# First phase of a binarised-convolution block: centring in pairs with rings of four, reordered first operations, batch statistics aggregated in two parts

## The reference, cut to what matters

```python
x = x + conv_block(_ln_c(x))          # _ln_c: subtract the mean over channels, divide by the deviation
# conv_block:
xa = sign(x)                          # only the sign of the centred x matters
wc = clip(w - mean(w, over input channels), -1, 1)
alpha = mean(abs(wc), per output channel)
y = conv3x3(xa, sign(wc) * alpha, padding 1) + b
mean, var = y.mean((0, 2, 3)), y.var((0, 2, 3))     # over all 32 images
y = relu((y - mean) * rsqrt(var + 1e-5) * gamma + beta)
# then, per image: tokens t (3136 x 128)
t = t + ffn(layernorm(t))             # a router picks the best half of the tokens, a two-layer MLP runs, gated
```

## Time and profile before

| what | value |
|---|---|
| median of 3 runs | 2134.3 us (2131.57 to 2134.45) |
| the profiled execution's own time | 2142.42 us |
| its span | 2140.6 us |
| PE busy | 1998.0 us, 93% of the span |
| DVE busy | 1671.8 us, 78% |
| ACT busy | 1211.8 us, 57% |
| POOL busy | 934.4 us, 44% |
| mean rate of the DMA | 125 GB/s |

### The profile page before, as it was taken

The page is one execution under the profiler, slowest core; times in us unless marked ns, Lnnn a source line. Parts: engine busy times, 40 slices in busy tenths (PEclk is TensorE's granted clock), DMA queues, the critical chain, the costliest instruction groups (busy, mean ns, idle before and its releaser), DMA issues.

```text
span 2140.6 us, 35882 instructions
## 1 busy us (share of the span) xinstructions
PE 1998.0 (93%) x9515; PEld 1015.2 (47%) x9515; DVE 1671.8 (78%) x4759; ACT 1211.8 (57%) x2030; POOL 934.4 (44%) x714
## 2 busy tenths in 40 slices
PE   6999999996799999999999999999999999999995
PEld 3555555553344444544444444444444444444442
DVE  6777777775688888888888888888887888888875
ACT  3444444443466565666665666666666656666652
POOL 1000000002456555666565565556655656555543
PEclk9999999998899999999999999999999999999998
DMA  4343444443123333333333333332333333333213
GB/s 162 136 180 140 175 153 162 164 151 135 51 87 122 115 120 130 117 112 139 111 120 125 110 127 123 118 128 110 119 132 111 119 125 128 110 123 119 103 69 123
DMA packets 68726, 267.91 MB, mean 125 GB/s; under 512 B 22352, under 2 KB 27184, under 8 KB 64688
## 3 DMA queue, kind: packets, MB, share of 16 engines
q1 hardware_dynamic: 55264, 214.90, 27.5%
q10 hardware_dynamic: 13392, 52.29, 6.6%
HBM read 188.08 MB, written 77.87 MB: 124 GB/s over the span
## 4 chain that ended last, share of the span: by engine, by line
PE 47%; DMA 10%; SPq 6%; DVE 5%; issue 4%; POOL 1%; ACT 1%; ACTq 0%; POOLq 0%; DVEq 0%
PE ps L955 23%; PE ps L944 6%; DMA y<-y_int 5%; PE ps L946 5%; PE ps L945 5%; PE ps L900 5%; SPq L371 4%; DMA w_row<-wrow 3%; DMA wse<-w_row 3%; PE ps L933 2%; SPq L377 1%; DVE base L720 1%; ACT hs L500 1%; DVE rms L697 1%; DVE rms L694 1%
## 5 line engine op out<-in xcount | busy, mean ns | idle before, releaser
L955 PE MATMUL ps<-hs,w_c 128*128 128x448 f32 x1792 | 765.7, 554 | 0.6 <-ACT yo L510 0.6
L500 ACT ACTIVATE hs<-ps,b1c,undo 128x448 f32<-128x448 f32 x896 | 609.8, 719 | 127.4 <-PE ps L946 120.5
L871 PE MATMUL ps<-yo,cwT 128*128 128x448 bf16 x2016 | 425.3, 356 | 0.0
L955 PEld LDWEIGHTS ps<-hs,w_c 128*128 128x128 f32 x1792 | 314.0, 191 | 209.5 <-issue 176.0
L412 POOL TENSOR_TENSOR xb<-xb,zr 128x448 f32<-128x448 f32 x224 | 261.3, 1168 | 271.8 <-ACT zr L528 270.4
L417 POOL TENSOR_TENSOR tl<-tr,th 128x448 f16<-128x448 f32 x224 | 243.5, 1088 | 308.6 <-PE ps L946 192.7
L944 PE MATMUL ps<-th,w_h 128*128 128x448 f16 x896 | 318.4, 355 | 19.5 <-ACT hs L500 19.5
L946 PE MATMUL ps<-th,w_l 128*128 128x448 f16 x896 | 316.3, 353 | 0.0
L945 PE MATMUL ps<-tl,w_h 128*128 128x448 f16 x896 | 316.3, 353 | 0.0
L424 POOL TENSOR_TENSOR yo<-yo,base 128x448 f32<-128x448 f32 x224 | 279.7, 1255 | 77.1 <-DVE yo L797 77.1
L510 ACT ACTIVATE yo<-ps,cols 128x448 f32<-128x448 f32 x224 | 141.8, 633 | 237.9 <-PE ps L955 237.5
(11 more groups left out here) (125 smaller groups left out, 2355.1 us busy)
## 6 DMA issues: line engine op xcount, KB each, us to landing
xb<-x SPq DMA_DIRECT2D x31, 1568.0 KB, 7.5
xb<-x SPq DMA_DIRECT2D x33, 896.0 KB, 4.7
gate_all<-gate_row ACTq DMA_DIRECT2D x32, 896.0 KB, 4.4
result<-yo SPq DMA_DIRECT2D x32, 896.0 KB, 3.5
y_int<-y SPq DMA_DIRECT2D x32, 784.0 KB, 3.7
xb<-x SPq DMA_DIRECT2D x33, 672.0 KB, 4.4
gate_all<-gate_row ACTq DMA_DIRECT2D x32, 672.0 KB, 5.6
result<-yo SPq DMA_DIRECT2D x32, 672.0 KB, 3.0
```

The lines of the kernel that those rows point to most:

```text
L500: nc.scalar.activation(hs[(b + slot) % 2][:, j, :], ps[:, H_BANK + j, 0:T], ACT.Gelu_apprx_tanh, bias=b1c[:, j:j + 1], scale=undo[:, 1:2]) ...
L871: last = M(bank, cwT[:, t, :], sg[b][:, c * ROWS + dy:c * ROWS + dy + ROWS, dx:dx + SIDE], start=t == 0, stop=t == TAPS - 1)
L955: last = M(bank, w2_c[:, j, :], hs[(b + c) % 2][:, j, :], start=first, stop=final)
```

## The change

Three things are done, all in phase one and behind it.

1. The rings of xh and xl and the centring banks get four places, addressed by the chunk alone (c % 4); the banks are 0, 1, 4 and 5. ring_free gives the count of centrings (or signs) after which a place is free. newly_due names the chunks that are centred, and signed, after convolution c: none after an even c, two after an odd one, one after c = 6. DVE's order of splits stays as it was.
2. The start: PE centres chunks 0 and 1 ahead of the weights' transposes (which now use the convolution's banks), chunks 2 and 3 behind them, chunks 4 and 5 after the first convolution and 6 after the second. ACT's Abs moves behind the first four signs.
3. The statistics of images 0 to 29 are aggregated ahead of the last image's share of DVE's phase; behind it only the last two images' 14 chunks are. Six small operations join the two parts into one mean and variance.

```diff
+RING = 4
+        bn_early, bn_late, bn_apart = sm[:, 10:12], sm[:, 12:14], sm[:, 14:15]
+        EARLY = n_img - 2
-        xh = [sb(f"xh{b}", [C, T], f32r) for b in range(2)]
-        xl = [sb(f"xl{b}", [C, T], f32r) for b in range(2)]
+        xh = [sb(f"xh{q}", [C, T], f32r) for q in range(RING)]
+        xl = [sb(f"xl{q}", [C, T], f32r) for q in range(RING)]
-        CEN_BANK, CONV_BANK = 0, 2
+        CEN_BANKS, CONV_BANK = (0, 1, 4, 5), 2
+        def newly_due(c):
+            return (c - 1, c) if c % 2 else (c,) if c == NCH - 1 else ()
+
+        def ring_free(n, c):
+            if c >= RING:
+                return n * NCH + c - RING + 1
+            return (n - 1) * NCH + (c + RING if c + RING < NCH else c) + 1
...
         (ACT)
-            nc.scalar.activation(cwa, cwc, ACT.Abs, accum_out=abs_sum).then_inc(abs_summed, 1)
...
-                nc.scalar.activation(cwT[:, t, :], ps[:, t % 2, 0:C // 2].bitcast(bf16),
+                nc.scalar.activation(cwT[:, t, :], ps[:, CONV_BANK + t % 2, 0:C // 2].bitcast(bf16),
...
-                bank = CEN_BANK + (b + c) % 2
+                bank = CEN_BANKS[c % RING]
...
-            for c in range(NCH):
+            for c in range(RING):
                 sign(0, 0, c)
+            nc.scalar.activation(cwa, cwc, ACT.Abs, accum_out=abs_sum).then_inc(abs_summed, 1)
...
+                    if is_int(n) and n == 0 and c < 2:
+                        for k in (range(RING, NCH - 1), range(NCH - 1, NCH))[c]:
+                            sign(0, 0, k)
                     if has(n + 1):
-                        sign(n + 1, 1 - b, c)
+                        for k in newly_due(c):
+                            sign(n + 1, 1 - b, k)
...
         (DVE)
-                wait_count(dve, centred, g - 1)
-                V.tensor_copy(xh[(b + c) % 2][:, :], cut(xb[b], c)).then_inc(xh_ready, 1)
+                wait_count(dve, centred, ring_free(n, c))
+                V.tensor_copy(xh[c % RING][:, :], cut(xb[b], c)).then_inc(xh_ready, 1)
...
-            pairs(dve, phase1, 3, n_img - 1, 3, n_img)
-
+            pairs(dve, phase1, 3, n_img - 1, 3, n_img - 1)
+
+            dve.wait_ge(bn_taken, EARLY * NCH)
+            V.bn_aggr(bn_early, bnst[:, 0:EARLY * NCH, :])
+            phase1(n_img - 1, (n_img - 1) % 2)
             batch_stats(n_img - 1, (n_img - 1) % 2, NCH - 1)
 
             dve.wait_ge(bn_taken, n_img * NCH)
-            link(V.bn_aggr(bn_mv, bnst[:, :, :]))
+            link(V.bn_aggr(bn_late, bnst[:, EARLY * NCH:n_img * NCH, :]))
+            share = EARLY / n_img
+            link(V.tensor_tensor(bn_apart, bn_early[:, 0:1], bn_late[:, 0:1], ALU.subtract))
+            V.scalar_tensor_tensor(bn_mv[:, 0:1], bn_apart, share, bn_late[:, 0:1], ALU.mult, ALU.add)
+            link(V.scalar_tensor_tensor(bn_apart, bn_apart, share, bn_apart, ALU.mult, ALU.mult))
+            V.tensor_scalar(bn_early[:, 1:2], bn_early[:, 1:2], share, None, ALU.mult)
+            link(V.tensor_tensor(bn_late[:, 1:2], bn_late[:, 1:2], bn_apart, ALU.add))
+            link(V.scalar_tensor_tensor(bn_mv[:, 1:2], bn_late[:, 1:2], 1.0 - share, bn_early[:, 1:2], ALU.mult, ALU.add))
...
         (PE)
-                wait_count(pe, signed, g - 1)
-                bank = ps[:, CEN_BANK + (b + c) % 2, 0:T]
+                wait_count(pe, signed, ring_free(n, c))
+                bank = ps[:, CEN_BANKS[c % RING], 0:T]
...
-            for c in range(NCH):
+            pe.wait_ge(tables_ready, 2)
+            for c in range(2):
+                centre(0, 0, c)
+            pe.wait_ge(cw_signed, 1)
+            for t in range(TAPS):
+                wait_count(pe, cw_ready, t - 1)
+                nc.tensor.transpose(ps[:, CONV_BANK + t % 2, 0:C // 2].bitcast(bf16), cws[:, t, :],
+                                    ident_b[:, :]).then_inc(cw_transposed, 1)
+            pe.wait_ge(cw_ready, TAPS)
+            for c in range(2, RING):
                 centre(0, 0, c)
 
             def phase1(n, b):
                 for c in range(NCH):
                     conv(n, b, c)
+                    if is_int(n) and n == 0 and c < 2:
+                        for k in (range(RING, NCH - 1), range(NCH - 1, NCH))[c]:
+                            centre(0, 0, k)
                     if has(n + 1):
-                        centre(n + 1, 1 - b, c)
+                        for k in newly_due(c):
+                            centre(n + 1, 1 - b, k)
```

More of the change, by code:

```diff
@@ L556, in split @@
             def split(n, b, c):
-                g = n * NCH + c
                 if is_int(n) and n == 0:
@@ L563, in split @@
                     dve.wait_ge(x_in_s[b], (n - b) * 8 + 16)
-                wait_count(dve, centred, g - 1)
-                V.tensor_copy(xh[(b + c) % 2][:, :], cut(xb[b], c)).then_inc(xh_ready, 1)
+                wait_count(dve, centred, ring_free(n, c))
+                V.tensor_copy(xh[c % RING][:, :], cut(xb[b], c)).then_inc(xh_ready, 1)
             def split_low(n, b, c):
                 dve.wait_ge(xh_ready, n * NCH + c + 1)
-                V.tensor_tensor(xl[(b + c) % 2][:, :], cut(xb[b], c), xh[(b + c) % 2][:, :].bitcast(f32),
+                V.tensor_tensor(xl[c % RING][:, :], cut(xb[b], c), xh[c % RING][:, :].bitcast(f32),
                                 ALU.subtract).then_inc(split_ready, 1)
@@ L846, in _ @@
             M = nc.tensor.matmul
[L847 to L853, removed]
             def centre(n, b, c):
@@ L858, in centre @@
                 pe.wait_ge(split_ready, g + 1)
-                wait_count(pe, signed, g - 1)
-                bank = ps[:, CEN_BANK + (b + c) % 2, 0:T]
-                M(bank, centre_r[:, :], xh[(b + c) % 2][:, :], start=True, stop=False)
-                M(bank, centre_r[:, :], xl[(b + c) % 2][:, :], start=False, stop=True).then_inc(centred, 1)
+                wait_count(pe, signed, ring_free(n, c))
+                bank = ps[:, CEN_BANKS[c % RING], 0:T]
+                M(bank, centre_r[:, :], xh[c % RING][:, :], start=True, stop=False)
+                M(bank, centre_r[:, :], xl[c % RING][:, :], start=False, stop=True).then_inc(centred, 1)
             def conv(n, b, c):
```

## The result

The changed kernel takes 2124.1 us (median of 8 runs, 2118.7 to 2127.3) against 2134.4 for the kernel before (8 runs beside them, 2129.7 to 2140.3): the medians lie 10.3 us apart. The ratio of the two is given as 0.9943 with a 95% interval of 0.9928 to 0.9958; by it the kernel is 12.2 us faster (9.0 to 15.4), so the size of the gain is known to some 3 us only. Its profiled execution took 2127.27 us for a span of 2125.5, 15.1 less than the one of before.

A forecast was written before the change was run, and what follows sets the result against it. TensorE (PE) was taken as the bound, busy without a gap in phase one, leaving its ends and a small stream excess. Savings of 5.8 + 1.0 + 3.75 = 10.6 us gave 2123.7 us, range 2119 to 2128.5.

The forecast's parts named there:

- Start: Beginning of phase one: Abs later and chunks centred ahead of the transposes, first convolution near 19.6; saves 5.8 us.
- the bounds by the clock: At the start: saving 6.2 us if the clock rises early, 4.8 if all 17 matmuls run slow.
- Middle: Steady stream of phase one: pairing centrings shares the step back to the convolution, some 0.01 us a pair; saves 1 us.
- rival (a): Mid-phase: changing between matmul kinds costs, not loads, so pairing halves the excess, saving 4.1 us there; 2120.6 us, chance 0.12.
- Nothing starves: Mid-phase: DVE's splits and ACT's signs keep up with pairs, since splits have more than a chunk (1.7 us) in hand.
- Junction: Between the phases: most aggregation done early, the first ReLU then waits for y's load; saves 3.75 us.
- One sign: Junction, expected in the changed profile: the large aggregation near 497, the small one under 0.6 us behind the last statistics.
- After it: Second phase: unchanged, moves as a whole from the first ReLU; zero, plus or minus 2 us for the clock.
- the sign that was named for it: Second phase: the forecast is wrong if its length from the first ReLU changes by over 2 us.
- (b): Start and head of second phase: the clock gives part of the gain back; 5.8 us saved, 2128.5 us, chance 0.08.
- (d): Start and junction: other waits hold both ends, half their gain is lost; 2129.5 us, chance 0.08.
- Slow rival (c): Mid-phase: a pair exposes one whole weight load, 0.19 us, 17.7 us in all; 2142.4 us, chance 0.04.

The follow-up runs named there:

- rings_only: The kernel before with only the rings and banks enlarged to four, old start and one aggregation kept; ratio to before 0.9989.
- old_start: The changed kernel with the old start: Abs first, all seven chunks of image 0 centred and signed behind the transposes; ratio to before 0.9958.
- early_y: The changed kernel with the first image's y loaded ahead of the last image's store; ratio to before 0.994.
- four_three: The changed kernel with four chunks centred after convolution 3 and three after convolution 6; ratio to before 0.9933.
- prep_spread: The changed kernel with DVE's preparation for the second phase dealt out one operation a chunk over images 0 to 4; ratio to before 0.9942.
- combined: The changed kernel with the edits of prep_spread, early_y and four_three together; ratio to before 0.992.
- before_again: The kernel before, unchanged, profiled once more; first ReLU at 519.85 us, 1623.3 us from there to the end.
- agg_only: The kernel before with the two-part aggregation of statistics alone; ratio to before 0.9984, 3.4 us.

## Why the prediction was right

The forecast was 10.6 us less, 2123.7; measured were 2124.1, 10.3 us less by the medians and 12.2 by the ratio. Step by step:

- **Start, 5.8 predicted.** 6.2 in the first profile, and 5.8 on average over the profiles (43.4 against 37.6). The first convolution starts at 19.93 where 19.6 was said, and the bounds by the clock were needed: the three profiles of the changed kernel lie 5.2 to 6.3 us ahead of that 43.4. The size was right, but the account of it was incomplete. The prediction compared the whole start before with the whole start after and never asked which part brings what. With the old order and larger rings alone 4.1 us are there (rings_only), 1.25 of them because the clock has risen before the first convolution. The reordering brings the rest: the first y store comes at 37.0 to 38.2 in the five profiles with the new start and pairs, against 39.15 in old_start, so 0.9 to 2.2 us by where the clock rises, 1.6 on average.
- **Middle, 1 us predicted.** The mechanism was right in kind and mis-sized: 2.0 us (0.067 an image), and two images became 0.13 us shorter where at most 0.1 was allowed. The step back to the convolution was taken as 0.01 us a pair and is 0.022 for each change-over spared (there and back). The other half of the excess stays with the centring matmuls, so rival (a), with 4.1, was further off on the other side. That it is their loads was argued from the rows and is not shown; that it doesn't depend on the grouping is. The rule of the Trainium skill (TensorE: Matmul & The Clock Gate, "LDWEIGHTS (loading the stationary operand)") that speaks for (a) fails on the load itself, 0.19 us in the rows again.
- **A term that was left out.** "Nothing starves" was argued from DVE's mean share in mid-phase, and the images at the front were not looked at. There DVE's preparation makes PE wait, 3.1 us at image 3 and 1.0 at image 1. Centring later shrinks these waits to 2.1 and 0.6, 1.4 us in the profile.
- **Junction, 3.75 predicted.** 3.8 in the first profile and 3.7 on average, with the load of y as the new releaser. The coefficients alone would have given 4.8; the six operations took 0.9 instead of 1.2. early_y confirms the bound from the other side. One sign was placed wrongly: the large aggregation was to come near 497 and runs from 486.5 to 492.3, ahead of the last image, and nothing waits for it.
- **After it, zero with 2 us either way.** The head of the second phase runs at low clock again; the length of the phase varies more than was allowed for, by 8 us between profiles. So the sign that was named for it, a change of over 2 us, could not tell anything: two profiles of the kernel before differ by 2.2.
- **The sum.** With the terms as measured (5.8, 2.0, 1.4 and 3.8) it would be 13.0 us up to the ReLU; the first pair of profiles has 13.4. The averages have 12.3, with 5.8 for the start, 2.0 for the pace, 0.8 for the waits (one of the three lost 1.7 to the clock at image 3) and 3.7 for the junction. The forecast was short by 1.0 in the pace and by the waits that it left out; the measured 12.2 by the ratio is near these 12.3. That the medians lie 10.3 apart, so close to 10.6, is luck.
- **Rivals (b) and (d).** The clock took no more at the start than the 1 us of its bound, and both ends came: the first convolution at 19.9, the ReLU 5.3 us behind the last store. What (b) adds in the second phase is the open point above.
- **Slow rival (c).** The loads in a pair start 0.20 apart and nothing is exposed. In four_three, with eight centring matmuls in a row, they still do.

## What to carry to other kernels

When a ring is enlarged and an order is changed in one edit, run the ring alone: at the start of a pipeline depth lets the producer run ahead while the consumer is still busy elsewhere, and here that was most of the gain at the start. In the steady state it brought nothing; there only the grouping of like matmuls counted, some two hundredths of a microsecond for each change-over spared. Look for one mark an image (a store, a release) before assuming a steady pace: one late block of small operations on another engine cost 3.1 us here, as much as 140 such change-overs, and an idle stretch can cost again through the clock.

## What the runs showed of the hardware

- The 4-byte weight loads of 0.19 us are hidden behind matmuls of 448 columns even eight in a row, but a change from one kind of matmul to the other and back costs 0.022 us each time, the same at three and at five spared an image (15.025, 14.96 and 14.91 us an image).
- Behind an idle stretch of PE in an otherwise full stream the clock may fall or not: after the wait of 2.85 us it did in two of five profiles, after two waits of 0.8 in two of five. Where it fell, image 3 took 1.5 to 1.7 us more. With the idle time removed image 3 didn't have it (prep_spread and combined, one profile each).
- At the start the clock, read from the pitch of the matmuls, rose earlier where PE had no waits: with the seven chunks of image 0 centred in a row from 18.9 us on, the matmuls are at their faster pitch of 0.20 us by 23.4 (rings_only, old_start); with waits between them they were still at 0.37 us when the first convolution began at 26.6 (before, before_again, agg_only).
- The aggregation of statistics costs in proportion to its input with a small start: 6.22 us for 1344 numbers, 5.83 for 1260, 0.53 for 84.
